# Deformable convolution on one core: the four corners are added in pairs on VectorE, and the two halves are added on TensorE while they are turned

## The reference, cut to what matters

```python
x = x + deformable(_gn(x), ...)      # layer 0
x = x + conv3x3(_gn(x), ...)         # layer 1

# layer 0, for each of 9 taps and each pixel, on 128 channels:
om = conv3x3(x, w_offset) + b_offset             # 27 planes: dy, dx, mask
py, px = pixel + tap + (dy, dx)
cols = corner(y0, x0, (1-ly)*(1-lx)) + corner(y0, x0+1, (1-ly)*lx) \
     + corner(y0+1, x0, ly*(1-lx))   + corner(y0+1, x0+1, ly*lx)
out = einsum('bckhw,ock->bohw', cols * sigmoid(mask), w_conv) + b_conv
y = relu(batchnorm(out))
```

## Time and profile before

| | |
|---|---|
| time, median of 3 runs | 948.8 us (947.56 to 950.48) |
| span of the profiled execution | 1061.3 us |
| mean granted TensorE clock in it | 0.780 |
| PE, busy share of the span | 72% |
| DVE | 76% |
| POOL | 63% |
| ACT | 36% |
| DMA software queue (the gathers) | 169.91 MB, 55.8% of 16 engines' span |
| gathers (L377) | 648, 947 ns each |

### The profile page before, as it was taken

How to read it: one execution, slowest core, us unless ns; L and a number is a source line. 1 busy time by engine, 2 the same in 40 slices (tenths; PEclk the granted TensorE clock), 3 DMA queues, 4 the chain that set the end, 5 groups by cost and what they waited for, 6 DMA issues and landing times.

```text
span 1061.3 us, 8955 instructions
## 1 busy us (share of the span) xinstructions
PE 763.8 (72%) x2436; PEld 354.9 (33%) x2436; DVE 803.4 (76%) x1533; ACT 378.9 (36%) x1026; POOL 669.4 (63%) x731
## 2 busy tenths in 40 slices
PE   6787777676766867666768667674776676579998
PEld 5342222322222222222223223221222222267776
DVE  3788788787878778786878778786888787867664
ACT  2333334433333335333424334332433333343320
POOL 3666666666666666666666666666666667635661
PEclk9677677778768668977867867976878775579999
DMA  8666666666666666666566665666666666630111
GB/s 290 185 171 185 187 191 185 176 189 184 185 178 188 186 183 189 189 189 182 166 185 191 189 187 169 186 186 181 181 186 189 186 188 189 175 113 23 51 50 56
DMA packets 56245, 181.38 MB, mean 171 GB/s; under 512 B 11012, under 2 KB 12036, under 8 KB 55812
## 3 DMA queue, kind: packets, MB, share of 16 engines
q0 software_dynamic: 51840, 169.91, 55.8%
q1 hardware_dynamic: 3924, 10.32, 2.6%
q10 hardware_dynamic: 432, 0.59, 0.2%
HBM read 176.06 MB, written 4.72 MB: 170 GB/s over the span
## 4 chain that ended last, share of the span: by engine, by line
POOL 39%; issue 16%; DVE 16%; PE 14%; another core or an unknown queue 10%; DMA 3%; ACT 2%; DVEq 0%; POOLq 0%; ACTq 0%
POOL g L377 39%; DVE g L858 5%; DMA g<-corner_table,idx 3%; DVE PA L870 2%; DVE PA L872 2%; PE TP L564 2%; PE PA L564 2%; PE CO L564 2%; DVE acc L874 2%; PE OMT L432 2%; PE TP L484 1%; PE VU L564 1%; PE OMT L564 1%; PE CO L472 1%
## 5 line engine op out<-in xcount | busy, mean ns | idle before, releaser
L377 POOL DMA_INDIRECT g<-corner_table,idx x648 | 613.5, 947 | 327.5 <-issue 188.9
L472 PE MATMUL CO<-cols,wcs 128*128 128x384 f32 (+1 forms) x504 | 261.2, 622 | 123.2 <-issue 64.7
L644 ACT ACTIVATE PA<-g,wt 128x128 f32<-128x128 f32 x642 | 203.0, 357 | 400.2 <-DMA g<-corner_table,idx 171.5
L858 DVE TENSOR_TENSOR g<-g,PA 128x1152 f32<-128x1152 f32 (+1 forms) x217 | 291.3, 1342 | 68.6 <-DMA g<-corner_table,idx 58.9
L432 PE MATMUL OMT<-xn,woff 128*27 128x384 f32 (+2 forms) x450 | 208.4, 576 | 43.1 <-DVE wt L828 21.7
L484 PE MATMUL TP<-ident,acc 128*128 128x128 f32 x648 | 145.1, 344 | 118.5 <-DVE acc L874 60.3
L472 PEld LDWEIGHTS CO<-cols,wcs 128*128 128x128 f32 x504 | 94.1, 241 | 285.8 <-issue 186.0
L484 PEld LDWEIGHTS TP<-ident,acc 128*128 128x128 f32 x648 | 92.4, 173 | 261.0 <-DVE acc L874 114.5
L870 DVE TENSOR_TENSOR PA<-g,PA 128x384 f32<-128x384 f32 x214 | 120.3, 562 | 59.6 <-ACT PA L644 22.9
L872 DVE TENSOR_TENSOR PA<-g,PA 128x384 f32<-128x384 f32 x214 | 120.3, 562 | 18.1 <-DVE PA L870 7.6
L874 DVE TENSOR_TENSOR acc<-g,PA 128x384 f32<-128x384 f32 x214 | 118.4, 553 | 15.2 <-DVE PA L872 4.9
(11 more groups left out here) (132 smaller groups left out, 545.8 us busy)
## 6 DMA issues: line engine op xcount, KB each, us to landing
g<-corner_table,idx POOLq DMA_INDIRECT x648, 3.4
out_dram<-x SPq DMA_DIRECT2D x16, 288.0 KB, 2.1
x<-x_dram SPq DMA_DIRECT2D x3, 1152.0 KB, 7.6
x<-x_dram ACTq DMA_DIRECT2D x3, 192.0 KB, 4.0
x<-x_dram SPq DMA_DIRECT2D x3, 192.0 KB, 3.8
wconv<-wconv_dram SPq DMA_DIRECT2D x1, 576.0 KB, 5.0
w<-w_dram SPq DMA_DIRECT2D x1, 576.0 KB
grid<-grid_dram SPq DMA_DIRECT2D x1, 162.0 KB, 4.1
```

The lines of the kernel that those rows point to most:

```text
L377: pl.indirect_dma_start(out=g[:, k, t].rearrange("p q c -> p (q c)"), out_offset=None, in_=tab_d, in_offset=bass.IndirectOffsetOnAxis(ap=i ...
L472: last = nc.tensor.matmul(co_bank(c, t)[:, t * P:t * P + size], wcs[:, c // CHUNKS % 2, k, :], cols[:, s % TURNS, n * P:n * P + size], sta ...
L644: last = nc.scalar.activation(first[:, n] if s < LAST_SUMS else g[:, k, t, 0, :], g[:, k, t, 0, :], ACT.Copy, scale=wt0[:, c % 2, t, k:k + 1])
L858: nc.vector.tensor_tensor(corners[:, :, 1:4, :], corners[:, :, 1:4, :], weights[:, :, 1:4].unsqueeze(3).to_broadcast([P, size, 3, P]), ALU ...
```

## The change

VectorE treats all items as the last three were treated, and stops after the pair add: one instruction adds corners 0 and 1 to corners 2 and 3, all in `g` in SBUF. The second add and the buffers `acc` are gone. TensorE adds the two halves: for every unit it does two ordinary float32 matmuls, with a half of `g` as the stationary operand and the identity as the moving one, into the same columns of bank TP, where the second accumulates. ScalarE scales corner 0 in place in `g` and no longer waits for VectorE's last item. `sum_step` counts two an item, and GpSimd's extra wait at the start of chunk 1 is on `turned`, because TensorE now reads `g` too.

```diff
-SUMS, TURNS = 5, 3
+TURNS = 3
+SUM_STEPS = 2
...
                         if first_item(c - 1) + used > first_item(c) + i - LEAD:
-                            pl.wait_ge(sum_step, (first_item(c - 1) + used + 1) * 4)
+                            pl.wait_ge(turned, first_item(c - 1) + used + 1)
...
-                pe.wait_ge(sum_step, (s + 1) * 4)
+                pe.wait_ge(sum_step, (s + 1) * SUM_STEPS)
...
-                for n in range(len(units)):
-                    last = nc.tensor.transpose(TP[s % 2][:, n * P:(n + 1) * P], acc[:, s % SUMS, n, :], ident[:])
+                for n, (k, t) in enumerate(units):
+                    for half in range(2):
+                        last = nc.tensor.matmul(TP[s % 2][:, n * P:(n + 1) * P], g[:, k, t, half, :], ident[:], start=(half == 0), stop=(half == 1))
                 last.then_inc(turned, 1)
...
-                if 0 < s < LAST_SUMS:
-
-                    act.wait_ge(sum_step, 4 * s)
                 for n, (k, t) in enumerate(items(c)[i]):
-                    last = nc.scalar.activation(first[:, n] if s < LAST_SUMS else g[:, k, t, 0, :], g[:, k, t, 0, :], ACT.Copy, scale=wt0[:, c % 2, t, k:k + 1])
+                    last = nc.scalar.activation(g[:, k, t, 0, :], g[:, k, t, 0, :], ACT.Copy, scale=wt0[:, c % 2, t, k:k + 1])
...
                 dve.wait_ge(scaled, s + 1)
-                dve.wait_ge(sum_step, 4 * s + 1)
-
-                some = first[:, 0:size]
-                if s >= LAST_SUMS:
-
-                    nc.vector.tensor_tensor(corners[:, :, 0:2, :], corners[:, :, 0:2, :], corners[:, :, 2:4, :], ALU.add).then_inc(sum_step, 2)
-                    dve.wait_ge(sum_step, 4 * s + 3)
-                    nc.vector.tensor_tensor(acc[:, s % SUMS, 0:size, :], corners[:, :, 0, :], corners[:, :, 1, :], ALU.add).then_inc(sum_step, 1)
-                    return
-                nc.vector.tensor_tensor(some, corners[:, :, 1, :], some, ALU.add).then_inc(sum_step, 1)
-                dve.wait_ge(sum_step, 4 * s + 2)
-                nc.vector.tensor_tensor(some, corners[:, :, 2, :], some, ALU.add).then_inc(sum_step, 1)
-                dve.wait_ge(sum_step, 4 * s + 3)
-                nc.vector.tensor_tensor(acc[:, s % SUMS, 0:size, :], corners[:, :, 3, :], some, ALU.add).then_inc(sum_step, 1)
+                dve.wait_ge(sum_step, SUM_STEPS * s + 1)
+                nc.vector.tensor_tensor(corners[:, :, 0:2, :], corners[:, :, 0:2, :], corners[:, :, 2:4, :], ALU.add).then_inc(sum_step, 1)
```

More of the change, by code:

```diff
@@ L98, in all_items @@
     return [(c, i) for c in range(ALL) for i in range(len(items(c)))]
-LAST_SUMS = len(all_items()) - 3
 def last_use(c, unit):
@@ L172, in build @@
         mixed = g[:].rearrange("p k t q c -> p (k t q c)")[:, 0:MIX * PW * HALF].rearrange("p (m r w) -> p m r w", m=MIX, w=HALF)
-        acc = sb("acc", [P, SUMS, TILES, P])
         cols = sb("cols", [P, TURNS, CP])
@@ L227, in build @@
         PA = (ps("PA0"), ps("PA1"))
-        first = PA[0][:, 0:CP].rearrange("p (u c) -> p u c", c=P)
         wt = PA[1][:, 0:2 * 4 * TILES * 9].rearrange("p (n q t k) -> p n q t k", n=2, q=4, k=9)
```

## The result

The changed kernel takes 992.5 us in the median of four runs (981.49 to 1000.13), the kernel before 949.59 us in four runs beside it. The ratio is 1.036, with a 95% interval of 1.0334 to 1.0386: slower. The ratio rests on the two fastest runs, 981.49 and 986.88 us; the other two, 998.12 and 1000.13 us, count as slow runs, and the profile shown is of the last. The changed kernel's runs lie wider apart (19 us) than those before (3 us). The profiled execution's own span is 998.4 us, 1.7 us under the time of the same run, so here the profile adds nothing to the time.

The account below looks back on a forecast made before the run. The prediction took GpSimd's issue of gathers as the bound. From 948.8 us it added 27 us for delayed gathers and 4 us for TensorE waits, small terms cancelling, giving 980 us, range 948 to 1025 us.

Parts of the forecast that it names:

- The bound: Whole gather stream: GpSimd issues gathers one after the other, 0.947 us each plus 0.30 us issue, a 1.25 us pitch.
- 6 us of real waits: Timed kernel before: 6 us of real waits besides 16 us ahead, 809 us of gathers and 118 us behind.
- VectorE's adds: Each item: three adds become one of 0.958 us, saving 0.72 us, 155 us in all, off the path; gain 0.
- What the new add does to the gathers: Gather starts: a gather reading indices in its first 0.05 us waits while VectorE streams two SBUF operands; otherwise runs free.
- I take the middle, 27 us, 0.13 us an item: Gathers delayed by the new add: cost between 0 and 55 us over the items, taken as 27 us.
- the chance phase: Rival for gathers meeting the add: once disturbed they never find back, 0.256 us every item; 1004 us, chance 0.14.
- The calm stretch: Profile before, around 236 us: the add's streaming fits between index reads; if all items did this, cost 0.
- the term of 4 us: GpSimd's waits for TensorE's longer turn that get through despite the room: 4 us.
- The rival with a cold TensorE: TensorE's turn becomes the bound if over 28% of items run cold; 1000 to 1070 us, chance 0.22.
- The small ones: Chunk 1 wait, at most 0.9 us later once, and kernel end, about -1 us: they cancel.
- No change: Rival: streaming slips between index reads nearly always, or contention is worth less; 949 us, 947 to 951, chance 0.14.
- faster: Rival: the 6 us, if waits for VectorE's adds, vanish and index reads aren't met; 941 to 945 us, chance 0.06.

Follow-up runs that it names:

- the kernel before with LEAD 6: Kernel before with only LEAD raised from 4 to 6, GpSimd two items further ahead; the base for comparing spans: 947.79 us, ratio 0.9997.
- The experiment with 0.2 us more: Changed kernel plus a useless 128-element VectorE instruction ahead of each pair add, starting it about 0.2 us later: 969.55 us, ratio 1.0226.
- TensorE's part alone: Kernel before, VectorE's adds kept, TensorE turning acc by two accumulating float32 matmuls a tile with half the identity, replacing one transpose: 954.07 us, ratio 1.0056.
- the version with an operand in PSUM: Changed kernel with the pair add replaced by two 384-element adds, each with one operand in PSUM; TensorE adds corners 2 and 3: 950.75 us, ratio 1.0018.

## Why the prediction came out as it did

*The bound* was right: GpSimd's issue of gathers, at 0.947 + 0.30 us. The table above is its proof. It was right too that the timed kernel doesn't have the pauses of the profile before. They are not in every profile, though: in the timelines of the changed kernel and of all nine experiments GpSimd has between 0 and 12 gaps longer than usual, 10 us at most in sum, and the kernel before, with another LEAD, spans 946.3 us. The "6 us of real waits" were put too high. In every run the time is 1.7 to 1.9 us over the span, and the longer gaps of the kernel before with LEAD 6 come to 3 us.

*VectorE's adds*: 0.961 us for a priced 0.958; what they save is idle time ahead of L853, now 245 us. It is worth nothing, as said.

*What the new add does to a gather* was right as a mechanism, from three sightings: the meeting is decided at the gather's start, the add holds up a gather from about 0.05 us after its own start on, and a gather under way is not harmed. The table by place of start shows it, and the count for L853 shows that an operand in PSUM does no harm. "A maximum near 1.7 us" was 1.72. That the gather reads its indices just then fits, but was not tested.

*The size of that term* was off. The term is the sentence "I take the middle, 27 us, 0.13 us an item", and the middle of 0 to 55 had no row behind it. In the profiled run it is 51.6 us, 0.24 an item. The other runs left no trace; if they too lost by their gathers alone, the two fastest lost some 34 us (0.036 of 949.6). The profiled run is near the chance phase's 55 us, but not by its terms: 106 gathers were delayed, 0.49 an item where it had 0.64, and each by 0.48 us in the mean where it had 0.40. Gathers met the add less often and earlier in it. The calm stretch, where nothing meets, does occur, but the choice gave it too much weight. That a long gather moves those behind it against the landings already under way is a reason that no run tests. The experiment with 0.2 us more shows how sharp the phase is: 15 us against the two fastest runs, 23 against the median. It would also explain why the runs of the changed kernel spread over 19 us and those before over 3; this is only argued.

*TensorE*: the term of 4 us was too large for the changed kernel, and about right for TensorE's part alone, which cost 5. The 3.5 us in the profile are seven gaps, five of them the usual 0.30 us (in total, times, longest):

```profile
POOL g L374 <- PE TP L482: 3.5, 7, 1.4
```

All gaps over 0.4 us come to 3.8 us beyond the usual, against 3.0 in the kernel before with LEAD 6, so the term is about 1 us. The waits that were to get through did not. VectorE's earlier end is enough for that, for the version with an operand in PSUM, which has no long gathers in its adds, spans only 1.8 us more than the base. Twelve records take 1.60 us from first to last in the timeline, 1.42 by the price in the prediction. The rival with a cold TensorE fell, as the clock was 0.985. Its "44% of the time was cold" came from the one profile with pauses, too; the timed runs before had 0.82 to 0.83, which makes some 35%.

*The small ones* at the end of the kernel come to half a microsecond: 117.4 us from the last gather, for 117.9. The one at chunk 1 was not looked at apart.

The sum, 980 us, is 1.3% under the median; the chance phase, 1004, was the nearer of the two for the profiled run (1000.13) and 980 for the fastest (981.49). Both were in the range. That 980 came as near as it did is in part luck: the contention was put too low, by some 7 us for the two fastest runs and by 25 for the profiled one, and TensorE's waits 3 us too high. "No change" and "faster" fell with the result itself.

## What to carry to other kernels

When GpSimd issues a stream of indirect DMAs and sets the pace, look at what VectorE reads while it issues: an instruction with both inputs in SBUF can hold up the next gather for most of its own length (0.77 of 0.96 us here), whatever it saves on VectorE. An operand in PSUM took the cost away here, and three shorter instructions most of it. Before crediting a saving, ask which engine has no idle time, and what the new form shares with it.

## What the runs showed that I had not expected

- The clock. TensorE had a granted clock of 0.78 to 0.83 in the three profiled kernels with transposes (0.780, 0.792, 0.832) and 0.974 to 0.995 in all kernels with matmuls in their place. TensorE's part alone shows it: only the turn is different, and the clock is 0.982. Whether it is the kind of instruction or the fuller engine that does it, no run tells apart. It gave nothing back in time, as TensorE isn't what holds the kernel.
- A useless VectorE instruction made a kernel faster by 23 us in the median, because it moved another by 0.2 us.
- A VectorE instruction of 1.10 us in three parts costs the stream of gathers 8 us, one of 0.96 us in one part 52 (both in the profiled run).
